# TensorE's order within an attention slot: two ring items ahead of the first score tile, then tile, item, tile, item

## What is computed

```
x = x + attention(layernorm(x))
x = x + ffn(layernorm(x))

attention: scores = q k^T / 4, times decay_mask[h, |i - j|]      (2 decays per head, mixed)
           probs  = softmax(scores);  out = probs v;  out = out Wo^T + bo
ffn:       W1, W2 quantized to -1, 0, 1;  relu(x W1^T + b1) W2^T + b2     (256 -> 1024 -> 256)
```

## Time and profile before

| what | value |
|---|---|
| median of three runs | 1915.69 us |
| the profiled execution, its own time | 1914.76 us |
| its span (first to last instruction) | 1912.9 us |
| TensorE matmul busy | 1793.8 us, 94% |
| VectorE busy | 1582.7 us, 83% |
| ScalarE busy | 1322.7 us, 69% |
| GpSimd busy | 782.0 us, 41% |
| mean granted TensorE clock | 0.968 of full speed |
| VectorE's reduces (L960) waiting for a ring item | 182.7 us, 439 times |
| weight loads of ring items (L1070) waiting for VectorE's reduces | 178.9 us, 529 times |
| TensorE's score tiles (L1101) waiting for exponentials | 8.8 us, 30 times |
| ScalarE's casts (L184) waiting for GpSimd's product | 60.7 us, 66 times |

### The profile page before, as it was taken

One profiled execution on the slowest core, in us unless ns is written; L12 is line 12 of the kernel. 1 busy time (PEld: TensorE's weight loads), 2 busy tenths in 40 slices (PEclk: granted clock), 3 DMA queues, 4 the chain that ended last, 5 costly groups with the idle time before them and its releaser, 6 DMA issues. The chain is left out here.

```text
span 1912.9 us, 32075 instructions
## 1 busy us (share of the span) xinstructions
PE 1793.8 (94%) x11794; PEld 747.2 (39%) x11794; DVE 1582.7 (83%) x3768; ACT 1322.7 (69%) x1518; POOL 782.0 (41%) x403
## 2 busy tenths in 40 slices
PE   5747999999999999999999999999999999985998
PEld 3422333333333333333333333333333333333666
DVE  5657888888888888888888888888888888865785
ACT  2353878786868686868686868686868686672555
POOL 3041818181808090909080818181818181002010
PEclk9865999999999999999999999999999999996999
DMA  7988363636363636363636363636363634407531
GB/s 126 289 258 195 71 157 88 157 88 157 86 159 86 157 88 154 92 154 90 154 90 155 89 154 91 154 91 154 93 154 94 154 94 110 112 17 184 149 91 34
DMA packets 132441, 242.61 MB, mean 127 GB/s; under 512 B 27696, under 2 KB 62896, under 8 KB 122032
## 3 DMA queue, kind: packets, MB, share of 16 engines
q1 hardware_dynamic: 129376, 237.84, 51.3%
q0 software_dynamic: 560, 2.36, 1.2%
q10 hardware_dynamic: 2352, 0.40, 0.1%
HBM read 69.08 MB, written 44.56 MB: 59 GB/s over the span
## 5 line engine op out<-in xcount | busy, mean ns | idle before, releaser
L933 ACT ACTIVATE probs<-tile 128x1024 f32<-128x1024 f32 x1024 | 999.5, 1024 | 299.6 <-PE tile L1098 171.4
L960 DVE TENSOR_REDUCE part_max<-ring 128x1 f32<-128x512 f32 x1536 | 964.0, 682 | 182.7 <-PE ring L1070 182.7
L1070 PE MATMUL ring<-k_stack,q_stack 96*128 96x512 f16 (+2 forms) x3072 | 661.1, 314 | 26.0 <-DMA q_stack<-lo 16.5
L1101 PE MATMUL tile<-q_stack,k_stack 98*128 98x512 f16 (+2 forms) x2560 | 588.4, 328 | 9.2 <-ACT probs L933 8.8
L1117 PE MATMUL acc<-probs,v_ones 128*32 128x512 f32 x4096 | 546.1, 605 | 0.0
L1101 PEld LDWEIGHTS tile<-q_stack,k_stack 98*128 98x128 f16 x2560 | 211.7, 98 | 570.5 <-ACT probs L933 342.3
L1070 PEld LDWEIGHTS ring<-k_stack,q_stack 96*128 96x128 f16 x3072 | 262.5, 99 | 311.3 <-DVE part_max L960 178.9
L870 POOL TENSOR_TENSOR diag<-diag,row_max 128x1024 f32<-128x1024 f32 x64 | 121.4, 1897 | 642.3 <-DVE row_max L973 642.3
L176 POOL TENSOR_TENSOR decayed<-qk,table_in 128x1024 f32<-128x1024 f32 x128 | 305.1, 2390 | 90.6 <-DMA table_in<-table_scratch 77.2
L962 DVE TENSOR_REDUCE part_max<-ring 128x1 f32<-128x384 f32 x512 | 278.9, 545 | 7.4 <-PE ring L1070 7.4
L190 POOL TENSOR_TENSOR lo<-decayed,hi 128x1024 f16<-128x1024 f32 x120 | 256.2, 2135 | 10.1 <-ACT hi L184 10.1
(11 more groups left out here) (142 smaller groups left out, 975.4 us busy)
## 6 DMA issues: line engine op xcount, KB each, us to landing
q_stack<-hi SPq DMA_DIRECT2D x320, 128.0 KB, 3.8
k_stack<-hi SPq DMA_DIRECT2D x128, 256.0 KB, 4.3
q_stack<-lo SPq DMA_DIRECT2D x160, 128.0 KB, 3.0
table_in<-table_scratch SPq DMA_DIRECT2D x64, 256.0 KB, 8.2
k_stack<-lo SPq DMA_DIRECT2D x64, 256.0 KB, 3.7
out_scratch<-heads_out SPq DMA_DIRECT2D x64, 256.0 KB, 3.1
v_scratch<-v_out SPq DMA_DIRECT2D x8, 1024.0 KB, 6.8
q_scratch<-q_out SPq DMA_DIRECT2D x32, 256.0 KB, 4.0
```

Of the source, the lines that this page charges most:

```text
L933: nc.scalar.activation(probs[:, t % 4], tile[t % 2][:].rearrange("p a b -> p (a b)"), ACT.Exp, scale=1.0 / (SCALE * SCALE * HEAD_DIM ** 0. ...
L960: nc.vector.tensor_reduce(out[:, k:k + 1], ring_bank(n), AX.X, ALU.max).then_inc(ring_free, 1)
L1070: last = nc.tensor.matmul(ring[:, n % RING, col:col + width], q_stack[h][0:STACK, q // UNIT_SLOTS, level, q0:q0 + P], k_stack[h][0:STACK, ...
L1101: last = nc.tensor.matmul(out, k_stack[h][:, level, kb * P:(kb + 1) * P], q_stack[h][:, half, level, col:col + width], start=bank not in s ...
```

## The change

In a slot, items 0 and 1 of the max pass are issued before tile A in place of behind it, ahead too of the two waits at the first slot of a unit. Item 2 moves from behind tile B to between the tiles. Item 3 stays behind tile B. No instruction is added or removed, and no wait is; the order on the other engines is as it was.

```diff
             def step(i, o, more):
                 for s in range(SLOTS):
                     ahead = more or s + LEAD < SLOTS
+                    if ahead:
+                        max_scores(s, s + LEAD, (0, 1), i, o)
                     if s % UNIT_SLOTS == 0:
                         u = s // UNIT_SLOTS
                         pe.wait_ge(rows_in, QUADS * (UNITS * i + u + 1))
                         pe.wait_ge(diag_ready, UNITS * i + u + 2)
                     scores(2 * s, o)
                     if ahead:
-                        max_scores(s, s + LEAD, (0, 1), i, o)
+                        max_scores(s, s + LEAD, (2,), i, o)
                     scores(2 * s + 1, o)
                     if s == SLOTS - 1 and o == STEPS - 1:
                         products(s - 1, o)
                     if ahead:
-                        max_scores(s, s + LEAD, (2, 3), i, o)
+                        max_scores(s, s + LEAD, (3,), i, o)
```

## The result

The changed kernel takes 1899.60 us (median of 4 runs, 1898.96 to 1900.08) against 1915.74 for the kernel before beside it (1913.74 to 1916.29): a ratio of 0.9917, 95% interval 0.9900 to 0.9935. It is 16.1 us faster, where 33.7 was forecast. The profiled execution took 1900.08 us, its span is 1898.2, the mean granted clock 0.967 against 0.968. The direction was right and the size was less than half of the forecast.

A forecast was written before the change was run, and what follows sets the result against it. The prediction took a loop of TensorE and VectorE, waiting for each other, as the bound. 15 x (0.49 + 2 x 0.82) = 32.0, plus 2.1, less 0.4 gave 33.7 off 1914.76: 1881 us, range 1871 to 1902.

The forecast's parts named there:

- The loop: Cross slot: item 0, VectorE's reduce, item 3, products and tile A form a closed loop of 2.93 us, falling to 2.76.
- The unheld price of items 2 and 3: TensorE, end of slot: 0.45 us without a stall, so 0.17 gained per cross slot and 0.11 per same slot.
- The turned maxima: Slot 6 of each unit: item 2 waits 0.30 us for the transpose's ring bank, a new cost of about 0.30 per unit.
- The first half of a step: Slots with ScalarE's casts: GpSimd's chain is not shortened, so the gain is only 0.46 in 13 slots, 0.49 in all.
- the chain's head start of 0.09: Slot 0's output copy comes about 0.1 us earlier; slot 10's cast starts at 34.28 relative to slot 0, before 34.37.
- The rival in which slot 0 hands its 0.44 on to the chain: ScalarE's lag reaches further, or cast slots stall TensorE more; first halves give nothing or lose: 1889 to 1896 us, 11%.
- waits less for exponentials in slots 9 and 12: First half of a step: TensorE's score tiles wait 1.9 us per step for exponentials, where it was 0.6.
- its total of tiles waiting for exponentials: Sign on the profile page: score tiles' waits for exponentials rise from 8.8 to some 28 us.
- The sum: Whole kernel: 15 steps x (0.49 + 2 x 0.82), 2.1 for the last step, less 0.4: gain 33.7 us.
- the prediction took off 0.4: First slots of attention, at half clock with TensorE the bound: two or three slots without a gain, 0.4 us.
- isn't the bound: Rival: VectorE becomes the bound if its reduces lose their overlap, slots of 2.80, about 1897 us, 12%.
- The rival that item 3's stall stays: The stall is item 3's weight load behind a full array, not the reduce, so it stays: 1912 to 1917 us, 5%.

The follow-up runs named there:

- e10: Order before, but VectorE's reduce of item 0 covers 256 of its 512 columns, TensorE's order untouched: 1891.81 us.
- e6: Second part alone against the kernel before: item 2 between the tiles, items 0 and 1 not ahead (A, 0, 1, 2, B, 3): 1920.01 us, ratio 1.0024.
- e7: Kernel after, with GpSimd's list beginning with products 2 and 3, which need only loaded data: 1881.52 us.
- e11: Order before, with GpSimd's list beginning with products 2 and 3, which need only loaded data: 1904.96 us.
- e4: Kernel before, with item 3 as one 512-column matmul in place of three: 1914.69 us.
- e1: Kernel after, with item 3 as one 512-column matmul in place of three, except in each head's last slot: 1899.26 us.
- e2: Kernel after, with item 3 as two 256-column matmuls in place of 256, 128 and 128: 1898.37 us.
- e3: Kernel after, with item 3 as four 128-column matmuls in place of 256, 128 and 128: 1899.29 us.
- e5: Kernel after, but item 2 back behind tile B (0, 1, A, B, 2, 3), the first part alone: 1897.49 us.
- e8: Kernel after, but order 0, A, 1, B, 2, 3 and GpSimd's list beginning with products 2 and 3: 1878.49 us, ratio 0.9807 to the kernel before.
- e9: Kernel after, without the products' own waits for exponentials where tile B already waited for the same or a later one: 1898.98 us.
- e12c: Kernel after, products' eight matmuls issued twice in 496 slots, by the order told the batches in a row: 2304.92 us.
- e13c: Kernel after, products' eight matmuls issued twice in 496 slots, by the order told the extra batch between tile A and item 2: 2416.82 us.

## Why the prediction missed

**The loop: right.** Item 0, reduce, item 3, products, tile A did set the cross slot of 2.93. e10 shows it from VectorE's side, e6 from TensorE's: without more distance from item 0 to item 3 nothing is gained. Item 3's wait is gone in the kernel after.

**The unheld price of items 2 and 3: wrong, and this is the step that failed.** The prediction put it at 0.45, from the 0.44 of items 0 and 1. It is 0.53: 0.44 of columns and 0.09 for going over to the products, which items 0 and 1 don't pay, since a score tile stands behind them. The stall that goes is thereby 0.09 in a cross slot and 0.03 in a same slot, in place of 0.17 and 0.11. The loop's own sum had hidden the error: it split the 0.33 from item 3's weight load to the products as 0.11 and 0.22, where the trace has the first matmul 0.01 behind its load, then 0.23 of columns and 0.09 for going over. That one term, 0.08 a slot, explains 15 x 16 x 0.08 = 19 us in the second halves alone, more than the miss of 17.6.

**The turned maxima: half right.** The wait is there, in slot 6 and at item 2. The new cost is 0.08 a unit and not 0.30: the matmul starts right behind the weight load, VectorE took the bank 0.34 behind the transpose and not 0.41, and with the slot's start 0.09 later in the new sum item 1 has no wait. The lowest value given was 0.22. This error went the other way: 15 x 2 x 0.22 = 6.6 us hid part of the first one, which is luck.

**The first half of a step: mechanism right, size 0.27 in place of 0.49.** GpSimd's chain sets it: the cast of slot 10 moved by 0.01 relative to slot 0, where 0.09 was forecast, and tile A of slot 12 by as much. e7 and e11 confirm the chain. Most of what is missing is the same term again. The products of slot 0 end only 0.03 earlier in the slot, not 0.11, so the output copy comes 3.13 behind the start of slot 0 where it was 3.16, and the chain's head start of 0.09 is not there. In slot 12 item 3 costs 0.31 and not 0.22. Together that is about 0.18 of the 0.22. The rival in which slot 0 hands its 0.44 on to the chain did not happen. With slots of 2.84 and 2.97 TensorE is less far ahead of ScalarE than forecast, and waits less for exponentials in slots 9 and 12: 1.2 us a step by the starts, where 1.9 was forecast. The page of the profile shows these waits badly: its total of tiles waiting for exponentials fell from 8.8 to 4.8 us, since it counts engine idle only; the 0.49 us from 974.45, when items 0 and 1 are through, to tile A at 974.94 stand there as 0.32, and tile A of slot 12 has no bracket, though it starts 0.72 behind item 0 in place of 0.44.

**The sum redone with the measured terms.** A unit gains 4 x 0.09 + 4 x 0.03 - 0.08 = 0.40. 15 x (0.27 + 0.80) + 0.9 for the last step = 17 us, against 16.1 between the medians and 14.7 between the two profiled executions. In these two the loop gives 16.6, and 2.5 are lost before slot 2 of the first step, where the prediction took off 0.4. How much of that is the change's stays open: slot 2 starts at 189.15 to 190.58 in the four traces whose slots begin with tile A and whose reduces are whole (before, e4, e6, e11), and at 190.29 to 192.36 in the eight with items ahead of tile A (after, e1, e2, e3, e5, e7, e8, e9).

**The rivals.** VectorE kept 0.28 of idle time in a cross slot and isn't the bound. The rival that item 3's stall stays came true in part: of the 0.18 that items 2 and 3 took over the 0.44 of their columns, 0.09 stayed. It is not at item 3's load, as that rival had it, but in front of the products. The clock didn't fall: the mean is 0.967, and from 210 to 1700 us the granted clock is 1.00 (2.4 GHz) in spite of the waits of 0.5 and 0.3 us ahead of tile A in slots 9 and 12. The Trainium skill's "TensorE: Matmul & The Clock Gate", section "HAM oscillation — how this bites in real kernels", describes an engine that waits for data longer than it works between two waits. The prediction read it more widely than that; nothing of the kind shows here.

## What to carry to other kernels

The unheld price of a group of instructions must be read where the same group stands in front of the same successor. The price of a neighbour of another kind (here 0.09 us in and about 0.1 out) isn't a stall, and no order with as many changes of kind wins it back; fewer changes would (0.226 us for each pair of ways, e12c against e13c). Where an engine's share of a loop is shortened, look first at the chain that holds it elsewhere: here the chain of another engine kept 7 us of the gain, and a new order at the head of its list gave back 18.

## What the runs showed of the hardware

- Going from 128-column f16 matmuls to 32-column float32 ones and back costs about 0.2 us (0.226 by the times of e12c and e13c). The weight loads of the second kind don't run ahead over the first, with a wait or without one (e9: load at 1017.56, the last of item 3's matmuls started at 1017.41). A 128-column float32 transpose between the same f16 matmuls pays nothing of the kind (962.57 to 962.96 for 896 columns).
- Four f16 matmuls of 128 columns with four weight loads cost what one of 512 columns costs in this place: 1899.29 us (e3) and 1899.26 (e1).
- VectorE's 512-element reduces last 0.682 us each and start 0.60 apart (three of them take 1.89), while TensorE writes the other ring banks.
